# Graph net on one core: three one-hot parts gathered side by side, TensorE waits renumbered, gathers ahead of scatters, and the sort's one-hots made a group earlier

## What is computed

```python
for l in range(3):                                   # L0: message net
    m = relu(concat([x[src], x[dst], ew]) @ edge_W[l] + edge_b[l])
    x = relu(concat([x, segment_sum(m, dst)]) @ node_W[l] + node_b[l])
agg = segment_sum(hW[etypes, src], dst)              # L1: relation net, 8 edge types
h = relu(sage(x, ...)); out = relu(sage(h, ...))     # L2: two mean aggregations
for l in range(2):                                   # L3: attention net, 2 heads
    scores = leaky_relu(s_h[src] + s_t[dst] + s_r[edge_type])
    A = 0.85 * segment_softmax(scores, src)
    for _ in range(3):
        Z = segment_sum(A[:, :, None] * Z[dst], src) + 0.15 * h[:, None, :]
```

## Time and profile before

| | |
|---|---|
| median of 3 runs | 14024.08 us (14017.4 to 14031.53) |
| profiled execution, whole / span of its instructions | 14034.0 us / 14032.2 us |
| TensorE busy, weight loads busy | 81%, 72% |
| VectorE, ScalarE, GpSimd busy | 77%, 37%, 18% |
| granted TensorE clock, mean over the span | 0.95 |
| sort, by its indirect DMAs | 250 to 1561 us |
| message net's three passes | 1743 to 2667, 2794 to 3652, 3778 to 4637 us |
| the two first spreads | 8442 to 9412 and 11625 to 12597 us |

### The profile page before, as it was taken

One profiled execution on the slowest core, in us unless ns is written; L12 is line 12 of the kernel. 1 busy time (PEld: TensorE's weight loads), 2 busy tenths in 40 slices (PEclk: granted clock), 3 DMA queues, 4 the chain that ended last, 5 costly groups with the idle time before them and its releaser, 6 DMA issues. The chain is left out here.

```text
span 14032.2 us, 473362 instructions
## 1 busy us (share of the span) xinstructions
PE 11396.0 (81%) x112719; PEld 10086.3 (72%) x112912; DVE 10845.1 (77%) x39414; ACT 5252.1 (37%) x19100; POOL 2474.9 (18%) x7659
## 2 busy tenths in 40 slices
PE   3444488899899689986665779999998779999998
PEld 2444377688788589975554339999998338999998
DVE  5444499688588378886564997779998997779998
ACT  1000022122122122235453237775454236775554
POOL 2777300000000000001110001112222001112222
PEclk9999999899899689999896999999998999999999
DMA  1111166443233011113231553332221553332222
GB/s 50 45 48 45 53 215 214 134 116 116 74 116 116 24 33 40 40 44 81 67 83 48 140 146 101 104 93 73 71 73 53 131 145 103 103 96 73 71 73 62
DMA packets 1206835, 1232.88 MB, mean 88 GB/s; under 512 B 218351, under 2 KB 1042800, under 8 KB 1206106
## 3 DMA queue, kind: packets, MB, share of 16 engines
q1 hardware_dynamic: 1180954, 1228.47, 31.5%
q0 software_dynamic: 25792, 3.35, 0.2%
HBM read 1115.06 MB, written 116.16 MB: 88 GB/s over the span
## 5 line engine op out<-in xcount | busy, mean ns | idle before, releaser
L1672 ACT ACTIVATE msgs<-G,share 128x64 f32<-128x64 f32 x6000 | 1397.1, 316 | 1343.5 <-PE G L1686 1343.5
L976 DVE TENSOR_SCALAR hot<-iota_row,place 128x128 f32<-128x128 f16 (+1 forms) x9000 | 1811.8, 266 | 2.6 <-POOL place L957 1.4
L968 DVE TENSOR_SCALAR hotT<-idx,iota_col 128x512 bf16<-128x512 f16 x4500 | 1315.4, 350 | 614.3 <-PE G L1111 557.7
L1686 PE MATMUL G<-u_b,hotT 128*128 x12000 | 1591.6, 276 | 50.0 <-DVE hotT L1620 50.0
L1053 PE MATMUL G<-table_m,hotT 128*128 x9000 | 1419.5, 248 | 226.3 <-issue 149.7
L1696 PE MATMUL S<-msgs,hot 128*128 128x128 f32 x12000 | 1586.2, 275 | 0.0
L1130 ACT CAST msgs<-G 128x384 bf16<-128x384 f32 x2250 | 1026.2, 481 | 1447.4 <-PE G L1111 1440.8
L1075 DVE TENSOR_REDUCE sums<-G 128x128 f32<-128x384 f32 x2250 | 1247.7, 555 | 376.9 <-PE G L1057 354.9
L1686 PEld LDWEIGHTS G<-u_b,hotT 128*128 128x128 f32 x12000 | 1467.0, 193 | 50.7 <-issue 50.7
L1696 PEld LDWEIGHTS S<-msgs,hot 128*128 128x128 f32 x12000 | 1462.1, 192 | 0.0
L1083 ACT ACTIVATE msgs<-sums 128x128 f32<-128x128 f32 x2250 | 702.6, 312 | 2002.3 <-DVE sums L1075 2002.3
(11 more groups left out here) (322 smaller groups left out, 20714.9 us busy)
## 6 DMA issues: line engine op xcount, KB each, us to landing
idx<-pos_rows SPq DMA_DIRECT2D x6375, 128.0 KB, 2.9
hotT<-hots_d SPq DMA_DIRECT2D x750, 256.0 KB
hots_d<-hotT SPq DMA_DIRECT2D x375, 256.0 KB, 3.1
key_b<-key_rows SPq DMA_DIRECT2D x62, 416.0 KB
ty_b<-type_rows SPq DMA_DIRECT2D x62, 416.0 KB
rows<-rel_rows SPq DMA_DIRECT2D x1500, 6.0 KB
ew_now<-ew_rows_d SPq DMA_DIRECT2D x1125, 3.0 KB
sorted_d<-recs,place POOLq DMA_INDIRECT x806
```

The lines of the kernel that those rows point to most:

```text
L968: op = eng.tensor_scalar(hotT[:, c % deep, n], idx[:, c, r], p.col[:, first:first + 1], None, ALU.is_equal)
L976: op = eng.tensor_scalar(hot[:, c % 2, q], p.row16[:], place[:, c % 2, q:q + 1], None, ALU.is_equal)
L1672: op = eng.activation(msgs[:, c % 2, 2 + j // HEADS, j % HEADS * D:(j % HEADS + 1) * D], G[c % 2][1][:, j * D:(j + 1) * D], ACT.Copy, scal ...
L1686: mm = eng.matmul(G[c % 2][b][:, k * W:(k + 1) * W], hotT[:, c % 2, q * P:(q + 1) * P], table[:, ds(dst_at(at, q, 24 * W), W)], start=True ...
```

## The change

Four edits. (1) In the sort, `step` is split in `hots` and `places`, and VectorE makes the one-hots of group g+1 before the places of group g. (2) In the message net's three passes TensorE issues both gathers and then both scatters; a gather waits for `taken` (VectorE has read the bank) and no longer for `made`; a scatter still waits for `made`. (3) In the first spread the three matmuls of `own` become one: its 64 columns already reach over the three parts, which stand side by side, so one matmul gathers all of them, ScalarE copies 12 numbers per edge, and VectorE adds them up in a new instruction (`add_up`). The fold stands between `add_up` and `bend`, and `lessen` directly behind `bend`. (4) The semaphores of the first spread are numbered so that TensorE's three waits ahead of a scatter compare with one register; the wait for relation rows moves from TensorE to VectorE (`hotT` waits for 48 instead of 32), and TensorE's wait of the gather for `made` is gone.

```diff
@@ sort_edges, VectorE
-                body(eng, step)
+                hots(0, 0, True)
+                hots(1, 1, True)
+                places(0, 0, True)
+                hots(2, 0, False)
+                places(1, 1, True)
+                with eng.Fori(1, S // 2 - 1) as i:
+                    hots(i * 2 + 1, 1, False)
+                    places(i * 2, 0, False)
+                    hots(i * 2 + 2, 0, False)
+                    places(i * 2 + 1, 1, False)
+                hots(S - 1, 1, False)
+                places(S - 2, 0, False)
+                places(S - 1, 1, False)
@@ edge_pass, TensorE (freed=taken in gnn_layer)
+                    if freed:
+                        for h in range(H if gathers else 0):
+                            ready(eng, freed[h], t + 1)
+                            gather(eng, c, h, at, env).then_inc(gathered[h].h, 1)
+                        for h in range(H if scatters else 0):
+                            ready(eng, made[h], t + 1)
+                            scatter(eng, c, h, was, env).then_inc(scattered[h].h, 1)
+                        return at
                     for h in range(H):
                         ready(eng, made[h], t + 1)
@@ first_spread, VectorE
+                def add_up(t, c):
+                    reach(eng, termed, te0, t + 1)
+                    eng.tensor_reduce(total[:, c % 2], terms[:, c % 2].rearrange("p k (i r) -> p k r i", r=2 * HEADS), AX.X, ALU.add
+                                      ).then_inc(totals.h, 1)
@@
                     if some(1):
-                        bend(t - 1, (c - 1) % 4)
+                        add_up(t - 1, (c - 1) % 4)
                     if some(4):
                         fold(t - 4, c, at)
                     if some(1):
+                        bend(t - 1, (c - 1) % 4)
                         lessen(t - 1, (c - 1) % 4)
@@ first_spread, ScalarE
-                    eng.copy(terms[:, c % 2], G[c][:].rearrange("p (k f) -> p k f", f=W)[:, :, D:D + 2 * HEADS]
+                    eng.copy(terms[:, c % 2], G[c][:].rearrange("p (k f) -> p k f", f=W)[:, :, D:D + 6 * HEADS]
@@ first_spread, TensorE
-                    arrived(eng, rel_in[c], r0[c], t, c, 16)
-                    reach(eng, made, m0, t - 3)
...
-                        for i in range(3):
-                            eng.matmul(to[:, D:2 * D], near[:, c % 2, q * P:(q + 1) * P],
-                                       s.own[:, ds(src_at(at, 24 * SMALL) + i * 2 * HEADS, D)], start=False, stop=False)
+                        eng.matmul(to[:, D:2 * D], near[:, c % 2, q * P:(q + 1) * P],
+                                   s.own[:, ds(src_at(at, 24 * SMALL), D)], start=False, stop=False)
...
-                    reach(eng, hots, h0, t + 1)
-                    reach(eng, folded, f0, t)
-                    reach(eng, made, m0, t + 1)
+                    reach(eng, hots, 0, now + 1)
+                    reach(eng, folded, 0, now + 1)
+                    reach(eng, made, 0, now + 1)
```

More of the change, by code:

```diff
@@ L545, in _, with hots @@
                 n = 11
-                def step(g, h, first):
+                def hots(g, h, first):
+                    if not isinstance(g, int) or g > 0:
+                        after(eng, hot, g)
                     after(eng, rows[h], 48 * ((g - h) // 2 + 1) if first else 24 * (g - h) + 48)
@@ L557, in step, with places @@
                     one_hot_columns(eng, dox[:, h], s.edge_cols[:, 1, ds(g * GRP, GRP)], p).then_inc(hot.h, 1)
+                def places(g, h, first):
                     after(eng, lookd, g + 1)
@@ L884, in src_at, with edge_pass @@
     return (words[0] >> 16).with_bounds(min_val=0, max_val=most)
-def edge_pass(p, s, rows, hot_dt, hot_parts, gather, scatter, vector, scalar, finish, extra=None, keep=None):
+def edge_pass(p, s, rows, hot_dt, hot_parts, gather, scatter, vector, scalar, finish, extra=None, keep=None, freed=None):
     ctx = ExitStack()
@@ L903, in edge_pass @@
         idx_in = [p.fresh("positions") for _ in range(4)]
-        stored = [p.fresh("hots_stored") for _ in range(4)]
+        stored = [p.fresh("hots_stored") for _ in range(4 if keep == "store" else 0)]
         placed, turned, hots = p.fresh("placed"), p.fresh("gather_hot"), p.fresh("scatter_hot")
@@ L987, in _ @@
                 eng.nop().then_inc(hots.h, 1)
+                for h in range(H if freed else 0):
+                    eng.nop().then_inc(freed[h].h, 1)
                 if keep != "load":
@@ L1095, in gnn_layer @@
                   extra=(s.ew_now, s.ew_rows),
-                  keep="store" if l == 0 else "load")
+                  keep="store" if l == 0 else "load", freed=taken)
 def parts_pass(p, s, row, tables):
@@ L1369, in first_spread @@
         idx_in = [p.sem(f"positions_{c}") for c in range(4)]
[L1370 to L1375, removed]
+        turned, hots, made, folded = (p.fresh(x) for x in ("gather_hot", "scatter_hot", "made", "folded"))
+        placed, shared, gathered, scattered, termed, bends, lessed, kept = (p.sem(x) for x in (
+            "placed", "shared", "gathered", "scattered", "termed", "bent", "lessed", "kept"))
+        hots.at, made.at, folded.at = 3, 3, 4
+        i0 = [x.at for x in idx_in]
         tu0, h0, pl0, sh0, sc0, f0, te0, b0, le0, k0 = (x.at for x in (
@@ L1433, in lessen @@
                     reach(eng, shared, sh0, t - 1)
-                    eng.tensor_tensor(less[:, c % 2], bent[:, c % 2], terms[:, c % 2, :, HEADS:2 * HEADS],
+                    eng.tensor_tensor(less[:, c % 2], bent[:, c % 2], total[:, c % 2, :, HEADS:2 * HEADS],
                                       ALU.subtract).then_inc(lessed.h, 1)
@@ L1464, in _ @@
                 scatter_hots(Q - 2, (Q - 2) % 4)
+                add_up(Q - 1, (Q - 1) % 4)
                 bend(Q - 1, (Q - 1) % 4)
@@ L1516, in step @@
                     pick(t, c)
+                for _ in range(3):
+                    eng.nop().then_inc(made.h, 1)
                 quarters(eng, step)
```

28 lines of the change are left out of this document (17 added, 11 removed).

## The result

The changed kernel takes 13509.04 us (median of 3 runs, 13507.32 to 13518.01) against 14024.08: a ratio of 0.9634, 95% interval 0.9612 to 0.9656. It is 515 us faster, where 364 were forecast and 13560 was the range's lower end. The profiled execution took 13518.0 us, with a span of 13516.2.

The account below looks back on a forecast made before the run. Bounds taken: GpSimd's ring in the sort, VectorE in message layer 0, TensorE fullest in layers 1 and 2 and bounding the first spread. 75 + 52 + 97 + 142 = 366 us, giving 13660 us; range 13560 to 13760.

Parts of the forecast that it names:

- the four terms: Forecast gains: sort 75 us, message layer 0 52 us, message layers 1 and 2 97 us, first spread 142 us.
- rival: Alternatives: removed matmuls dearer 0.10; VectorE binds first spread 0.16; layers 1-2 unmoved 0.12; sort gain lost 0.10; slower 0.02.
- may be held for that time too: Sort: GpSimd, no longer idle between `recs` and `tyT`, may lose those 0.91 us a group as well.
- So I take 2.16 − 0.91 = 1.25: Sort: wait saved less possible extra hold, in us a group; times 60 groups, 75 us.
- the ring: Sort: one-hots, lookup, places and DMAs follow each other in a cycle of 21.3 us, GpSimd its largest member.
- the rule of the Trainium skill: Sort: VectorE's port lock keeps GpSimd from writing DMA descriptors; by it the gain would be the stretched case, 23 us.
- A step without a wait takes 2.27 us: Message layer 0: step read from the timeline, against 2.46 us then; the difference is 0.19 us.
- I take three quarters: Message layer 0: share of the 0.19 us taken as gain, 0.14 × 375 = 52 us.
- the loop's turn: Message layer 0: what the rest of the 0.19 us a step was put down to, not counted as gain.
- two thirds: Message layers 1 and 2: share of 0.20 us idle a step taken as gain, 0.13 × 750 = 97 us.
- With two engines this close a step loses a little more than the larger: I take 2.40: First spread: TensorE at 2.36 us, VectorE 2.26 to 2.44, so a step of 2.40, gaining 142 us.
- nothing is gained: First spread: renumbered waits save TensorE a register instruction or so a step, covered by queued matmuls, so 0 us.

Follow-up runs that it names:

- The experiments on pieces: `tyT` cut into pieces of 208 columns: in the kernel before 14249.99 us, in the changed kernel 13423.48 us; with `soT` cut too, in the changed kernel, 13388.95 us.
- the two halves: The changed kernel with only the new order of gathers and scatters, 13660.35 us, and with only the gathers' wait for `taken`, 13574.20 us.

## Why the prediction was wrong

The links named were the ones that gave way, but three of the four terms came out above their own upper bounds. No rival happened: TensorE kept the first spread, layers 1 and 2 gained, the removed matmuls cost what the starts showed, the sort's gain was not taken back.

**Sort, 75 forecast, 144 measured.** The failed step is that GpSimd "may be held for that time too", from which came "So I take 2.16 − 0.91 = 1.25". The stretched part is 2.72 us a group before and 2.47 after: not 0.91 more but 0.25 less. The reason is in the kernel before already: I had read one stretched issue, which lasts 2.73 us and begins 0.14 us ahead of `tyT`. In every other group it begins earlier, 0.48 us ahead, beside `soT`, and lasts 3.08, as here (it ends at 740.62, 0.28 us behind `tyT`):

```profile
737.54 3.08 POOL L606 DMA_INDIRECT sorted_d<-recs,place  x1 [2.32 <-DVE recs L578]
```

```profile
737.02 1.07 DVE L550 TENSOR_SCALAR soT<-sb_b,iota_col 25x1664 f32<-25x1664 f16 x1 [0.23 <-issue]
738.02 2.32 DVE L552 TENSOR_SCALAR tyT<-ty_b,iota_col 128x1664 bf16<-128x1664 f16 x4
```

So the time beside `soT` was in the mean already. After the change the long issues last 2.86 and 3.03 us by turns, so they are no longer in sum than 2.73 and 3.08, and the price passes the forecast's upper bound: 2.16 us of wait plus 0.25 of stretching, 2.4 × 60 = 144. Why the stretching fell by 0.25 stays open. The wait itself was right, and so was what takes it over (VectorE waits for sends). My reading of the ring was wrong in one link, "with GpSimd its largest member". In the kernel before VectorE stands for TensorE's lookups and never for a send, so the ring was VectorE's and TensorE's work one after the other, and GpSimd only followed it. The experiments on pieces fit this: before, VectorE's 3.8 us more lengthened the group by 3.6, and the stretching of GpSimd's issues was free; after, GpSimd bounds, and all of it counts. On the rule of the Trainium skill that I had weighed ("SBUF — State Buffer", section "SBUF: two separate sides", a lock held for a whole instruction): the stretch falls from 2.47 to 0.86 us with shorter instructions of VectorE, as that rule would have it. But the two ends don't fit it each time. An issue of the changed kernel ended at 904.30, 0.44 us ahead of the end of `tyT`; that of the next group is shown behind it:

```profile
901.44 2.86 POOL L623 DMA_INDIRECT sorted_d<-recs,place  x1 [0.30 <-issue]
919.97 3.03 POOL L623 DMA_INDIRECT sorted_d<-recs,place  x1 [0.30 <-issue]
```

```profile
902.42 2.32 DVE L554 TENSOR_SCALAR tyT<-ty_b,iota_col 128x1664 bf16<-128x1664 f16 x4
```

The one of the kernel with `soT` in pieces ended 0.84 us behind it. And each of these issues stood through three or four of the instructions of `tyT`, where a lock held for one of them could have let it in between. What decides the moment was not found. As a reason against the edit the rule failed, since the same stretching was there before.

**Message layer 0, 52 forecast, 84 measured.** The term was mis-sized by two steps. "A step without a wait takes 2.27 us": the step from which I read this still held waiting, since part of each short wait hides in the overlap of VectorE's rows; without one it is 2.240, and 0.22 us were to be had instead of 0.19. And "I take three quarters", with "the rest is the loop's turn": the loop's turn costs VectorE nothing, the mean step over the whole stage is the 2.240. 0.22 × 375 = 83. That the wait would go, and that VectorE would then bound, was right. That ScalarE's link and the order both matter here is shown by the two halves.

**Message layers 1 and 2, 97 forecast, 99 measured.** Right in cause: the wait for ScalarE is nearly the whole of it, and the loop's own issue gap stayed. That the size fits so well is in part luck. The "two thirds" had no row behind it, the idle of the weight loads fell from 0.38 to 0.28 us and not to half as forecast, and the same code gained some 113 us in most of the other programs (passes of 802 and 801 us).

**First spread, 142 forecast, 188 measured.** Eight matmuls at 0.028 were right (0.029). The failed step is "With two engines this close a step loses a little more than the larger: I take 2.40". It lost nothing: TensorE's own 2.34 is the step, with VectorE at 2.15 of it, and even a second `add_up` on VectorE cost nothing in one of the two spreads and 13 us in the other. The allowance of 0.04 us a step was 30 us. The prices behind it were too high as well: `add_up` cost 0.11 to 0.14 us and not the middle between 0.13 and 0.31. Another 11 are "nothing is gained" for the renumbered waits (0.015 us a step): that TensorE's rows leave no gap was taken for proof that its waits are free, which is the same mistake as in layer 0. The last 5 us are in the roundings.

**The range.** The upper bounds of the four terms were 130, 71, 150 and 172 us: 523 in sum, 13501 us, and the range ended at 13560. I took a deduction from each bound and then treated the four as if their errors would cancel. But three of the four had one origin, caution against losses that did not come, and failed the same way; that put 13509 outside. A range down to 13501 would have held it by luck only: three terms passed their bounds, by 14, 13 and 16 us, and the fourth stayed 51 us below its own. The bounds themselves rested on waits read too small (layer 0, the renumbered waits) and on a stretching that was thought able only to grow (the sort).

## What to carry to other kernels

When a gain is bounded by a wait that is seen, deduct only what a row shows as left over, take the wait that is shown as the least and not as the most it can be, and if several terms carry the same kind of deduction, let the range reach to where all of them fail together. An engine whose rows leave no gap can still be waiting: compare the distance of starts between equal pairs of instructions, not the idle time. And find the bounding member before pricing its disturbances: the same stretching of GpSimd's issues was free before the change and cost 2.5 us of 18.9 after it, so one and the same cure (`tyT` in pieces of 208 columns) made the sort of the kernel before 218 us longer and that of the changed one 98 us shorter.

## What the runs showed of the hardware

An indirect DMA of 128 records takes GpSimd 0.96 us to issue and 0.30 us to the next. One that met VectorE's four `tensor_scalar` of 1664 16-bit columns took 2.7 to 3.3 us, and 3.3 to 4.1 where eight short ones of another tile came just ahead; with 32 of 208 columns in place of the four the mean issue fell from 1.148 to 1.024 us. Cutting costs VectorE 3.8 us (0.19 us for each of 32 pieces, 0.58 for each of 4). A bf16 matmul of 64 columns with its own weight load of 128 columns adds 0.029 us to a full TensorE stream (granted clock 1.00), though each load shows as 0.10 us and the stage's mean is 0.081 per matmul. Two reduces in VectorE's stream start 0.47 us apart where neither waits, and a delay of 0.17 us of the second shows as 0.09 us idle. A VectorE reduce of 48 elements to 16 per partition adds 0.11 to 0.14 us, though its row shows 0.20.
